# Latent and multi-head queries and keys projected with features on the partitions, and laid out by transfers through memory

## What is computed

```python
# latent attention: 16 heads of 16 content + 64 rotary features
c_q = x @ w_dq.T;  q_c = c_q @ w_uq.T;  q_r = c_q @ w_qr.T
c_kv = x @ w_dkv.T;  k_c = c_kv @ w_uk.T;  v = c_kv @ w_uv.T
k_r = x @ w_kr.T
q_r, k_r = _rope(q_r, k_r)          # y * cos + rot(y) * sin, rot swaps the two halves of 32
attn = softmax((concat(q_c, q_r) . concat(k_c, k_r)) / sqrt(80) + causal mask)
latent = (attn @ v) @ w_out.T
# the block
xn = _rmsnorm(x, w_ln1);  q, k, v = xn @ Wq.T, xn @ Wk.T, xn @ Wv.T      # 16 heads of 16
x = x + (causal softmax(q . k / 4) @ v) @ Wo.T
# then the best 2 of 8 experts for each token, silu(g) * u, down, added to x
```

## Time and profile before

| | |
|---|---|
| median of 3 runs | 900.93 us (898.07 to 901.34) |
| the profiled execution | 900.06 us |
| its span, first to last instruction | 898.3 us |
| TensorE busy, share of the span | 92% |
| VectorE, ScalarE, GpSimd busy | 68%, 56%, 44% |
| a batch of the attention, from one transpose of the latent maxima to the next | 72.6 us |

### The profile page before, as it was taken

One profiled execution on the slowest core, in us unless ns is written; L12 is line 12 of the kernel. 1 busy time (PEld: TensorE's weight loads), 2 busy tenths in 40 slices (PEclk: granted clock), 3 DMA queues, 4 the chain that ended last, 5 costly groups with the idle time before them and its releaser, 6 DMA issues.

```text
span 898.3 us, 18344 instructions
## 1 busy us (share of the span) xinstructions
PE 822.7 (92%) x6432; PEld 735.3 (82%) x6432; DVE 612.4 (68%) x2191; ACT 502.1 (56%) x1089; POOL 391.4 (44%) x538
## 2 busy tenths in 40 slices
PE   5889999999999999999999999988669999999980
PEld 3778988898897898888889889866459999999980
DVE  4976666767767676667776675762537878887854
ACT  2445466457347536536645744644237878787851
POOL 4632342344344344434434434414344565656640
PEclk9988999999999999999999999977769999999995
DMA  9000000000000000000000000122368999999836
GB/s 291 2 1 2 14 1 12 16 13 3 25 14 2 25 14 1 26 13 2 14 14 13 3 25 13 11 87 86 105 183 207 237 230 232 255 261 243 234 37 198
DMA packets 49871, 71.07 MB, mean 79 GB/s; under 512 B 12067, under 2 KB 36003, under 8 KB 49763
## 3 DMA queue, kind: packets, MB, share of 16 engines
q1 hardware_dynamic: 39060, 57.41, 20.8%
q0 software_dynamic: 9856, 12.13, 7.7%
q10 hardware_dynamic: 864, 0.36, 0.2%
HBM read 55.13 MB, written 14.81 MB: 78 GB/s over the span
## 4 chain that ended last, share of the span: by engine, by line
PE 76%; DVE 10%; ACT 5%; DMA 4%; issue 3%; POOL 1%; SPq 1%; POOLq 0%; ACTq 0%; DVEq 0%
PE ps L608 62%; PE ps L702 6%; PE ps L739 3%; DVE ps L1509 2%; ACT ex L1175 2%; DVE ps L1506 1%; PE ps L635 1%; DMA expert_rows<-yo,slot_of 1%; DMA ln<-in_w_ln 1%; PE ps L992 1%; PE ps L644 1%; DMA xg<-x_normalised,slot_of 1%; SPq L377 1%; DVE xr L1788 1%; DVE s_tok L1786 1%
## 5 line engine op out<-in xcount | busy, mean ns | idle before, releaser
L544 POOL TENSOR_SCALAR_AFFINE_SELECT ex<-ex 128x256 f32<-128x256 f32 x256 | 104.4, 411 | 232.1 <-ACT ex L1175 211.4
L608 PE MATMUL ps<-qt,kt 81*128 81x128 f32 (+2 forms) x768 | 166.6, 331 | 3.8 <-ACT ex L1175 2.0
L1175 ACT ACTIVATE ex<-ps 128x384 f32<-128x384 f32 x240 | 116.0, 492 | 95.0 <-PE ps L608 93.2
L522 POOL TENSOR_TENSOR ex<-ex 128x256 f32<-128x256 f32 x128 | 102.5, 801 | 110.3 <-DVE ex L1466 109.3
L1506 DVE CUSTOM_DVE_ANT_0 ps<-ps,mask 128x128 f32<-128x128 f32 x256 | 77.1, 301 | 92.2 <-PE ps L608 88.8
L608 PEld LDWEIGHTS ps<-qt,kt 81*128 81x128 f32 (+1 forms) x768 | 111.1, 197 | 15.8 <-issue 6.0
L1509 DVE CUSTOM_DVE_ANT_0 ps<-ps,mask 128x256 f32<-128x256 f32 x256 | 118.6, 463 | 0.0
L585 POOL DMA_INDIRECT expert_rows<-yo,slot_of x46 | 77.0, 1674 | 82.6 <-ACT yo L1310 55.1
L1347 DVE TENSOR_TENSOR wel<-raw,weh 128x768 fp32r<-128x768 f32 x92 | 87.7, 956 | 18.3 <-ACT weh L1045 18.3
L608 PE MATMUL ps<-wh,xth 128*128 128x320 f32 (+2 forms) x352 | 96.1, 355 | 4.4 <-DVE wl L1347 3.0
L1045 ACT ACTIVATE qt<-ps 80x512 f32<-80x512 f32 (+1 forms) x96 | 56.8, 592 | 61.5 <-PE ps L702 59.4
(11 more groups left out here) (160 smaller groups left out, 1914.3 us busy)
## 6 DMA issues: line engine op xcount, KB each, us to landing
raw<-in_w_experts SPq DMA_DIRECT2D x92, 384.0 KB, 4.5
mla_branch<-s_b SPq DMA_DIRECT2D x8, 256.0 KB, 2.1
expert_rows<-xn SPq DMA_DIRECT2D x8, 256.0 KB, 2.1
x_normalised<-otk SPq DMA_DIRECT2D x8, 256.0 KB, 2.1
xr<-in_x SPq DMA_DIRECT2D x1, 2048.0 KB, 10.4
s_tok<-mla_branch SPq DMA_DIRECT2D x4, 512.0 KB, 6.9
w_cols_raw<-in_w_cols SPq DMA_DIRECT2D x1, 1792.0 KB, 15.6
x<-expert_rows SPq DMA_DIRECT2D x3, 512.0 KB, 5.1
```

Source lines behind the costliest of these rows:

```text
L522: nc.gpsimd.tensor_tensor(t, t, swp[:, n % 2, :, :], ALU.add).then_inc(tokd, 1)
L544: nc.gpsimd.affine_select(a, a, [[0, 2], [1, P]], ALU.is_ge, zero, 0, -1).then_inc(exm, 1)
L608: return nc.tensor.matmul(o, a, m, start=start, stop=stop, skip_group_check=True, **k)
L1175: nc.scalar.activation(ex[:, h % (2 * G), :], ps[4 + h % 2][:, P:4 * P], ACT.Exp, scale=scale).then_inc(ex_, 1)
```

## The change

Queries and keys are projected with the features on the 128 partitions and the 256 tokens along the row, so that no transpose by TensorE is needed. A product is a **unit**: two times six matmuls of 256 columns, whose fixed operand is now the weights (`features`). A batch has 13 units in a fixed order (`UNITS`): nq, nk (content features of queries and keys, all heads), q0 to q3 and k0 to k3 (rotary features of four heads each, first halves in the first 256 columns of the bank, second halves in the other), mq, mk (multi-head), and v. They go to banks 0, 1, 4 and 5 (`BANK`). The columns of the weights are reordered on the host for it, and so are the tables of cosines and sines.

What happens to a unit: nq and nk are copied by ScalarE to a slot of `stg`, a ring of five slots of 128x512 (`keep_content`). A rotary unit is multiplied twice by VectorE (`products`, 128x512 each, the second with the halves swapped) and summed by GpSimd (`rope_sums`, 128x512, eight for a batch). mq and mk are scaled by VectorE with the reciprocal root mean square (`mha_scale`), rounded by ScalarE (`mha_high`), and VectorE takes the low part (`mha_low`). SyncE stores each slot to memory (`qk_d`, `mha_d`) and, when the stores have landed, loads it back with the features of one head on the partitions: `load_heads` fetches four heads of queries and of keys, 80 partitions by 4 KB each, and `load_mha` fetches `qt2` and `kt2` in eight transfers of 48 partitions by four rows of 1 KB. VectorE rounds the loaded latent queries and ScalarE the keys, 80x1024 at a time, four times a batch, into a ring of three (`qr`, `kr`).

P2 is gone, and so are `qs`, `ks`, their copies, and the copies out of the transposes. Of each set of maxima scores the first two heads stand ahead of the stage: M1's behind unit q3, the multi-head ones ahead of T1. In T1 and T2 the scores for the maxima are two heads ahead of the scores that go to the exponential. The transpose of the latent maxima (`max_t1`) stands behind head 15 of T2, ahead of its last two products with the values. The scatters of the chosen slots move from the end of T2 into the next batch's T1 on GpSimd.

The core of the diff:

```diff
+UNITS = ("nq", "nk", "q0", "k0", "q1", "k1", "mq", "mk", "q2", "k2", "q3", "v", "k3")
+BANK = dict(nq=0, nk=1, q0=4, k0=5, q1=0, k1=1, mq=4, mk=5, q2=0, k2=1, q3=4, v=5, k3=0)
 # TensorE
+            def features(o, c0):
+                k = 0
+                for w, a in ((wh, xth), (wl, xth), (wh, xtl)):
+                    for e in range(ET):
+                        i = mm(o, w[:, e, c0:c0 + P], a[:, e, :], k == 0, k == 2 * 3 - 1)
+                        k += 1
+                return i
             def stage_p1(b, after):
+                free = dict(q0=(ex1, 16 * b), k0=(ex1, 16 * b), q1=(nkd, 2 * b + 1), k1=(nkd, 2 * b + 2),
+                            mq=(roped, 8 * b + 1), mk=(roped, 8 * b + 2), q2=(roped, 8 * b + 3),
+                            k2=(roped, 8 * b + 4), q3=(m2p, 2 * b + 1), v=(m2p, 2 * b + 2), k3=(roped, 8 * b + 5))
...
-                    for j in range(G):
-                        t = nc.tensor.transpose(ps[2 + n % 2][0:HW, j * P:(j + 1) * P], tok[:, n % 4, j, 0:HW],
-                                                idf[:, :])
...
             def max1(b): head
+                    if h % G == 0:
+                        wait(pe, rkd, NG * b + h // G + 1)
+                        wait(pe, rrd, NG * b + h // G + 1)
 # in batch
-                stage_p2(b, after2)
                 if more:
+                    max2(b)(0)
+                    max2(b)(1)
+                    if not first:
+                        to_tokens()
...
+                    p1_with_m1(b + 1, {"nq": after_first, "nk": to_tokens, "q1": back, "mq": project})
+                    after = {5: lambda: project_v2(b + 1)}
 # SyncE
+            def stage_p1(b, between):
+                wait(sp, st1, 16 * b)
...
+                stage_content(b, 0)
+                stage_content(b, 1)
+                stage_rope(b, 0, 0)
+                stage_rope(b, 0, 1)
...
+                stage_rope(b, 1, 0)
+                load_heads(b, 0)
+                stage_rope(b, 1, 1)
+                stage_mha(b, 0)
+                load_heads(b, 1)
+                stage_mha(b, 1)
+                between()
+                stage_rope(b, 2, 0)
+                stage_rope(b, 2, 1)
+                stage_rope(b, 3, 0)
+                load_heads(b, 2)
+                stage_rope(b, 3, 1)
+                load_heads(b, 3)
 # ScalarE
             def rounded(b, g):
-                wait(act, qke, 16 * b + 10 + 2 * (g // 2))
+                wait(act, rd[g], 32 * (b + 1))
...
+                stage_p1(b + 1)
+                after = {1: lambda: rounded(b + 1, 2), 5: lambda: rounded(b + 1, 3),
+                         15: lambda: max_t1(b + 1)}
 # VectorE
+            def products(b, n):
...
+                nc.vector.tensor_tensor(stg[:, s, :, :], a, cos_t[:, :].unsqueeze(1).broadcast_to([P, 2, S]), ALU.mult)
+                nc.vector.tensor_tensor(prb[:, n % 2, :, :], a[:, ::-1, :], sin_t[:, :, :], ALU.mult).then_inc(roped, 1)
...
             def stage_p1(b, after):
+                for n in range(4):
+                    products(b, n)
                     after.get(n, lambda: None)()
+                mha_scale(b, 0)
+                mha_scale(b, 1)
+                mha_low(b, 0)
+                mha_low(b, 1)
+                after.get("low", lambda: None)()
+                for n in range(4, 8):
+                    products(b, n)
+                    after.get(n, lambda: None)()
...
             def batch: in it
+                    stage_p1(b + 1, {1: normalise, "low": kept, 5: lambda: rounded(b + 1, 0), 6: lambda: first_m1(b + 1),
+                                     7: lambda: rounded(b + 1, 1)})
```

640 lines of the change are left out of this document (330 added, 310 removed).

## The result

The change made the kernel **slower**: 931.37 us (median of 4 runs, 929.72 to 932.21) against 899.50 us for the kernel before in the same comparison (897.11 to 901.34). The ratio is 1.035, with an interval of 1.032 to 1.039. The forecast was 856 us, in a range of 836 to 886. The profiled executions have spans of 930.3 and 898.3 us, so the difference to explain is 32.0 us.

The account below looks back on a forecast made before the run. TensorE was taken to bound the kernel. Per batch, P1 2.4, T2 2.7, stretch 1.5 and T1 0.4 less 1.0 for the clock left 6.0; seven batches 42 plus start 2 gave 900.06 - 44 = 856 us, range 836 to 886.

Parts of the forecast that it names:

- the stretch to T1: Between the latent maxima's transpose and T1: 3.6 us instead of 5.1, 1.5 less, with the row landing last.
- the clock: In T2: TensorE's waits lose the full clock in most batches, taken as 1.0 us a batch.
- the sign of the start: Ahead of batch 0's maxima: between nothing and 6 us, 2 taken, and counted in the sum as a gain.
- TensorE's work: In P1, P2 and T2: 10 us less a batch with waits kept; P1's own work 23.4 us against 28.4.
- under 1.00 in T2 only: Sign to look for: the granted clock falls below 1.00 in T2 and in no other stage.
- the clock stays low: Rival: low through the rest of T2 and into P1's waits, 3.5 us a batch instead of 1.0; 873 us, chance 0.15.
- The walk through P1: P1, engine by engine: waits for VectorE make it 26.0 us, 2.4 less, not 5.0.
- that through T2: T2, engine by engine: ScalarE waits 2 and 2.7 us for loads; the stage becomes 14.8 us, 2.7 less.
- The period: Time of one whole batch: 66.6 us forecast; under 64 or over 70 would refute the walk.
- The hops: Trips through memory from P1's end to T1: a store lands after 2.1 us, two loads after 3.7.
- the slow rival: Four hops from k3's store to T1 each take 2 to 2.4 us more: 930 us; slower had chance 0.06.
- After batch 7: Last batch and experts: 0 us, since that batch has its own order and the experts are untouched.

Follow-up runs that it names:

- e3: The changed kernel with both the edit of e1 and the later roundings of e2: 900.17 us, ratio 1.004.
- e1: The changed kernel with even heads' row of maxima moved from row 48 to 112, so all heads contract 112 rows: 910.75 us, ratio 1.011.
- e5: e3 plus twenty matmuls whose result nobody reads, ahead of T1 of batch 0: 885.98 us, ratio 0.987.
- e6: e5 plus eight unread matmuls ahead of each of latent maxima heads 0, 8 and 12 in batches 1 to 7: 888.04 us, ratio 0.990.
- e10: e9 plus six unread matmuls ahead of latent maxima head 3 in T2 of batches 1 to 7: 873.97 us, ratio 0.975.
- e12: e10 plus four and three unread matmuls ahead of latent maxima heads 4 and 7 in T2 of batches 1 to 7: 865.32 us, ratio 0.965.
- e4: The changed kernel with stores and loads of multi-head queries and keys cut to 32 of 256 tokens: 922.74 us, ratio 1.026.
- e7: e5 with VectorE's seven pairs of normalising moved from the first P1 into T1 of batch 0: 881.04 us, ratio 0.982.
- e9: e7 plus eight unread matmuls ahead of latent maxima head 0 only, in P1 of batches 1 to 7: 884.90 us, ratio 0.985.
- e2: The changed kernel with roundings of groups 2 and 3 behind ScalarE's exponentials 5 and 9 and ahead of VectorE's maxima 7 and 11: 925.57 us, ratio 1.032.
- e8: The changed kernel plus only the twenty unread matmuls ahead of T1 of batch 0: 918.86 us, ratio 1.024.

## Why the prediction was wrong

Forecast and result lie 76 us apart in the spans (44 less, 32 more). They come from batch 0, 22.6 us (forecast 6.0 less, measured 16.6 more); from batches 1 to 6, 8.35 each, 50.1 together; from the start, 9.0; and 5.7 go the other way behind the last batch. Of the 8.35 a batch, T1 has 3.5, P1 2.9, T2 with its clock term 1.7 and the stretch to T1 0.2. So the steps that failed are T1's even heads, which had no term, the clock, which had 1.0 us in T2 and nothing in T1(0) and P1, and the sign of the start.

**TensorE's work: right in the products, wrong in what was costed at nothing.** P1's TensorE work was forecast at 23.4 us and is 23.68 where the clock held (e3, batch 2). The edit of `max2` had no term at all: its rows went from 128 to 48 for even heads and to 112 for odd ones, and the prediction doesn't mention them. T1 was 3.1 us longer for it and a little clock, and 21 us of the whole are the rows' (e1), which alone turns the forecast gain of 44 into 23.

**The clock: the mechanism was named and its size missed.** The sum had 1.0 us a batch in T2 and nothing elsewhere. Three places were missed:
- *T1(0)*. The sum counted batch 0 like the others. P2's transposes were costed only as work that goes. In the kernel before, the clock rose at 75.8 us, among them, ahead of T1(0); without them it stays at 0.50 for the whole stage, which costs 14 us (e5). That they were what raised it is read from this and from e5's twenty matmuls in the same place, where the clock rose at 79.7 us, 0.9 ahead of T1(0).
- *P1's waits*. P1 after is 26.82 us where the clock held (e3, batch 2: 23.68 us of work and 3.1 of waits) and 28.1 to 29.2 in the kernel after, where it did not. That the granted clock would be "under 1.00 in T2 only" was false; the fall in P1 costs 1.3 to 2.4 us.
- *T2*. At full clock 15.8 to 16.5 us (e6, e10, e12), at a broken clock 16.3 to 20.0.

The rival *the clock stays low* was closest in its mechanism, with "if T1 starts low too, 884". But it made 3 to 5 us of T2 and forgot P1, and T1(0) was an afterthought in it. By the Trainium skill (TensorE: Matmul & The Clock Gate, HAM oscillation) a loop whose bursts stand behind waits for a transfer, some 3 to 5 us each in its example, starts every burst low. The trace agrees only in part: TensorE's waits in T2 are 0.4 to 2.0 us here, e10 has the same ones once with and once without the fall, and those ahead of it were for VectorE. In the kernel after the fall did come in the T2 of every batch (0.80 to 0.90), as the prediction took from that page; in e10 it stayed away from three of six.

**The walk through P1 was nearly right, that through T2 only in its total.** With the clock held, P1 is 26.8 us (forecast 26.0), T2 15.8 (14.8), the stretch to T1 3.2 to 4.0 (3.6), and T1 with 112 rows 21.3 to 22.0 (21.2). `back` waits 1.15 us in P1 (1.1 forecast); the first latent maxima 1.95 (1.3). The period at full clock is 67.9 us in e12's batches 1 to 3, beside 66.6 forecast. But the 15.8 is of e10 and e12, which have the later roundings and the added matmuls; no run shows the T2 that was walked at full clock, and in the kernel after ScalarE stood 3.48 and 0.21 us ahead of its two roundings where the walk had 2 and 2.7. The hops were dearer than priced. SyncE's transfers from 292 to 306 us of the kernel after:

```profile
DMA packets 2614, 3.57 MB, mean 255 GB/s; under 512 B 207, under 2 KB 2256, under 8 KB 2612
...
latent_heads<-stg SPq DMA_DIRECT2D x4, 256.0 KB, 4.2
qt<-latent_heads SPq DMA_DIRECT2D x2, 320.0 KB, 3.2
kt<-latent_heads SPq DMA_DIRECT2D x2, 320.0 KB, 3.5
```

A store was priced at 2.1 us, from a store that ran nearly alone; here it landed after 4.2 in the median. The walk also let the loads of group 2 go out right behind q3's sum; they wait for the stores of q2 and k2, issued at 294.30 and 295.02 us and landed after 4.7 and 4.6, so they went out 2.6 and 3.4 us behind that sum. `stage_mha`'s stores, `store_s` and the rotary ones go out in the same few us, and with the bytes of the first reduced to an eighth the two landed after 3.3 and 3.0 (e4). The pair of loads landed 4.7 us after the first issue (299.06 to 303.75), priced at 3.7. GpSimd's sum was 1.39 rather than 1.3, and ScalarE's rounding 1.06, the upper of its two bounds. The argument against the slow rival, that the heavy piece lies in P1 and T2's hops escape it, was thus false: the load reaches over P1's end. The rival gave four hops 2 to 2.4 us more each; the store took up to 2.6 more and the pair of loads 1.0. But its verdict, 930 us, was reached by other causes: e4 gives the multi-head bytes on the transfers 8.6 of the 75 us between forecast and result, and T2 didn't grow at all (17.95 and 17.96 us). That the number fits is chance.

**The start.** The sum took 2 us of gain there, though every item that the passage names costs time; the maxima came 7.0 later. The pairs were priced at 1.9 us and six of seven took 1.7, so the price was right, but they were not added up: the walk asked whether TensorE's banks fill up and not what stands between VectorE and its first rounding. e7 gave 4.5 us back, all by which e5's maxima came later than those of the kernel before; the other 2.5 lie between the profiles of the kernel after and e5 (78.33 and 75.86), of which no edit tells.

**After batch 7** the forecast had 0 and the time is 5.7 us less: 4.3 of it ahead of the first matmul of the experts and 1.5 in the experts, which the change doesn't touch. The last batch has no P1 behind it, so P2's work may be saved there without a new wait. That is a reading; it was not tested.

Added up from the changed kernel to e12: rows 20.7, later roundings 10.6, T1(0)'s clock 14.2, the start 4.9, the clock in P1 and T2 15.7; 66.1 us of 931.4 (by the ratios, 7.0% or 63 us). That 865 us come near the forecast's 856 is luck in good part: the later roundings and the added matmuls are not in the change that was forecast, and e12's profile gains 8.5 of its 35.6 us behind batch 7, where the forecast had none, and 27.2 instead of 42 in the seven batches.

**What stays open.** Why the load of 64 rows or fewer isn't put under the 81-row matmul ahead of it is not shown, only that it isn't. In e9 five of the T2 of batches 1 to 6 ran at 0.74 and in e7 they ran at 0.8 to 0.9; there a P1 at full clock was followed by a worse T2, and no run tells why. Nor does one tell why e10's batches alternate, or what let the clock rise within T1(0) in e2. And the clock of T2 in batches 4 and 6 of e12 still falls.

## What to carry to other kernels

Before work is taken from TensorE, ask what clock the next stage starts at: a dense stretch that looks like overhead may be what pays for the stage behind it. A cost of zero for an edit of operand shapes is a term like any other and needs a row; here the cheaper-looking shape cost 21 us, and the whole clock term of the sum was 7. Price a transfer by one that had the same neighbours. Matmuls nobody reads can pay ahead of a long stage that would start at 1.2 GHz (e5, e8); in the short waits of a pipeline try them one place at a time, since e6 and e9 gained nothing and only e10 and e12 did.
